# State-space stage of a decoder layer: convolution taps read the projection's bank, SiLU by ScalarE's own function, more banks for the projection, another order of the scan

## What is computed

```
h = rmsnorm(x, ln1_w)
z, xs, Bs, Cs, dt = split(h @ w_in.T, [512, 640, 768, 1280])
xBC = silu(causal_conv4(concat(xs, Bs, Cs), conv_w) + conv_b)   # 768 channels, 4 taps
dt  = softplus(dt + dt_bias);   a = dt * -exp(A_log)            # 4 heads
L   = tril(exp(cumsum(a)[q] - cumsum(a)[k]))                    # one chunk of 128
Y   = ((C @ B.T) * L) @ (xs * dt) + D * xs                      # state before it is zero
x1  = x + ((Y * silu(z)) @ w_out.T)
```

## Time and profile before

| | value |
|---|---|
| median of 3 runs | 1024.9 us (1024.14 to 1027.17) |
| the profiled execution's own time | 1025.79 us |
| its span, first to last instruction | 1024.0 us |
| mean granted TensorE clock | 0.98 |
| PE busy | 973.0 us, 95% of the span |
| DVE busy | 597.0 us, 58% |
| ACT busy | 495.0 us, 48% |
| POOL busy | 411.2 us, 40% |

### The profile page before, as it was taken

How to read it: one execution, slowest core, us unless ns; L and a number is a source line. 1 busy time by engine, 2 the same in 40 slices (tenths; PEclk the granted TensorE clock), 3 DMA queues, 4 the chain that set the end, 5 groups by cost and what they waited for, 6 DMA issues and landing times.

```text
span 1024.0 us, 15445 instructions
## 1 busy us (share of the span) xinstructions
PE 973.0 (95%) x5010; PEld 806.2 (79%) x5010; DVE 597.0 (58%) x1361; ACT 495.0 (48%) x1380; POOL 411.2 (40%) x341
## 2 busy tenths in 40 slices
PE   4897999999999999899999999999999999999886
PEld 3664677788888888788888888888888888888772
DVE  3879465322212247566667666666666676657865
ACT  4634535122312245654655654655555555555544
POOL 3334646534334353343442442532623523533312
PEclk9999899999999999999999999999999999999995
DMA  6110115101110211011011020020110110100002
GB/s 214 42 42 0 42 42 167 55 7 61 61 61 4 99 62 55 22 42 42 21 41 41 20 82 0 20 82 0 26 77 0 61 41 12 50 0 0 1 1 83
DMA packets 12976, 45.58 MB, mean 45 GB/s; under 512 B 1617, under 2 KB 2257, under 8 KB 9873
## 3 DMA queue, kind: packets, MB, share of 16 engines
q1 hardware_dynamic: 12944, 45.20, 12.7%
HBM read 43.10 MB, written 2.10 MB: 44 GB/s over the span
## 4 chain that ended last, share of the span: by engine, by line
PE 86%; DVE 8%; issue 2%; ACT 2%; POOL 1%; DMA 1%; SPq 0%; ACTq 0%; DVEq 0%
PE bank L377 25%; PE bank L378 24%; PE bank L379 24%; PE bank L651 5%; PE bank L661 3%; DVE cbuf L1634 2%; PE bank L775 1%; PE bank L388 1%; DVE xbc L1650 1%; DVE bst L1810 1%; PE bank L638 1%; DMA res<-in_x 1%; PE bank L741 0%; DVE xn L1592 0%; DVE res L1710 0%
## 5 line engine op out<-in xcount | busy, mean ns | idle before, releaser
L377 PE MATMUL bank<-act_hi,w_hi 128*128 128x512 f32 x560 | 226.3, 404 | 4.2 <-ACT cbuf L875 2.3
L379 PE MATMUL bank<-act_hi,w_lo 128*128 128x512 f32 x560 | 220.3, 393 | 0.0
L378 PE MATMUL bank<-act_lo,w_hi 128*128 128x512 f32 x560 | 220.1, 393 | 0.0
L1503 POOL TENSOR_TENSOR pb<-pb,prec 128x512 f32<-128x512 f32 x64 | 66.7, 1042 | 310.1 <-DVE prec L1944 310.1
L1160 ACT ACTIVATE pb<-pb,nmax 128x128 f32<-128x128 f32 x256 | 99.7, 391 | 78.2 <-DVE nmax L1939 78.2
L377 PEld LDWEIGHTS bank<-act_hi,w_hi 128*128 128x128 f32 x560 | 106.4, 190 | 28.9 <-issue 7.5
L378 PEld LDWEIGHTS bank<-act_lo,w_hi 128*128 128x128 f32 x560 | 106.3, 190 | 23.4 <-issue 2.2
L379 PEld LDWEIGHTS bank<-act_hi,w_lo 128*128 128x128 f32 x560 | 106.1, 189 | 23.0
L377 PE MATMUL bank<-w_hi,ot_hi 128*128 128x512 f32 x256 | 105.0, 410 | 0.8 <-DVE res L1957 0.8
L379 PE MATMUL bank<-w_hi,ot_lo 128*128 128x512 f32 x256 | 100.9, 394 | 0.0
L378 PE MATMUL bank<-w_lo,ot_hi 128*128 128x512 f32 x256 | 100.4, 392 | 0.0
(11 more groups left out here) (193 smaller groups left out, 2105.8 us busy)
## 6 DMA issues: line engine op xcount, KB each, us to landing
raw_a<-in_w_q SPq DMA_DIRECT2D x8, 1024.0 KB, 4.8
raw_b<-in_w_o SPq DMA_DIRECT2D x8, 1024.0 KB, 4.8
raw_a<-in_w_gu SPq DMA_DIRECT2D x7, 1024.0 KB, 5.3
raw_b<-in_w_kv SPq DMA_DIRECT2D x8, 512.0 KB, 3.3
raw_b<-in_w_dn SPq DMA_DIRECT2D x7, 512.0 KB, 3.4
res<-in_x SPq DMA_DIRECT2D x8, 256.0 KB, 6.4
raw_b<-in_ctx_t SPq DMA_DIRECT2D x8, 256.0 KB, 3.6
xre<-in_x SPq DMA_DIRECT2D x2, 1024.0 KB, 6.8
```

Of the source, the lines that this page charges most:

```text
L377: mm(o, l_hi, r_hi, start=first, stop=False)
L378: mm(o, l_hi, r_lo, start=False, stop=False)
L379: return mm(o, l_lo, r_hi, start=False, stop=last)
L1503: TT(pb[:, jj % 2, :, :], pb[:, jj % 2, :, :], prec[:, jj % 2, :].unsqueeze(2).to_broadcast([P, GH, L]), ALU.mult).then_inc(p_norm, 1)
```

## The change

- **Taps.** `conv` reads the raw value from the projection's bank instead of `pre`. Since there is no zero column, a tap of shift s adds only to columns s to 127 of each sequence. ScalarE's copy into `pre` is gone, and `pre` with it. The halved weights and their setup go too.
- **SiLU.** ScalarE's own SiLU writes `xbc` from `cbuf` and `zt` from the bank. `conv_silu` and `z_silu` on VectorE are gone, as are the factors of two.
- **Banks.** The projection uses banks 0, 1, 4, 5 in the first half of the tokens and 0, 1 and for two steps 6 in the second, by the table `IN_BANK`. A convolution's bank is now free only when its taps are done (`conv_c`), where before it was free when ScalarE had read it (`conv_ev`).
- **Order.** `dt_in(0)`, `dt_out(0)` and `dt_out(1)` stand earlier on VectorE. On TensorE `in_step(18)` and `in_step(19)` stand ahead of `ssm1(4)`. The output steps, the residual additions and the pieces of the normalization in the second half are threaded in another order.

```diff
+        IN_BANK = [0, 1, 4, 5, 0, 1, 4, 5, 0, 1, 0, 1, 6, 0, 1, 6, 0, 1, 0, 1]
             def in_step(f):
-                if f >= 2:
-                    pn, pp = order[f - 2]
+                if f == 12:
+                    pe.wait_ge(dt_a, 2)
+                elif f >= 4:
+                    pn, pp = order[max(e for e in range(f) if IN_BANK[e] == IN_BANK[f])]
                     if pp < NCONV:
-                        pe.wait_ge(conv_ev, NCONV * pn + pp + 1)
+                        pe.wait_ge(conv_c, NCONV * pn + pp + 1)
                     else:
                         pe.wait_ge(z_out, NH * pn + pp - NCONV + 1)
...
             def in_evac(f):
-                    A(pre[:, q % 2, :, DCONV - 1:], bank[f % 2][:, :].rearrange("p (s n) -> p s n", s=HALF),
-                      ACT.Copy)
-                    A(cbuf[:, q % 3, :], bank[f % 2][:, :], ACT.Identity,
+                    A(cbuf[:, q % 3, :], bank[IN_BANK[f]][:, :], ACT.Identity,
...
-                    A(th[:, 0, :], bank[f % 2][:, :], ACT.Tanh, scale=0.5).then_inc(z_th, 1)
+                    A(zt[:, h, n * NTOK:(n + 1) * NTOK], bank[IN_BANK[f]][:, :], ACT.Silu).then_inc(z_out, 1)
-            def conv_tanh(q):
+            def conv_silu(q):
                 act.wait_ge(conv_c, q + 1)
-                A(th[:, 1 + q % 2, :], cbuf[:, q % 3, :], ACT.Tanh).then_inc(conv_th, 1)
+                A(xbc[:, q // NCONV, q % NCONV, :], cbuf[:, q % 3, :], ACT.Silu).then_inc(conv_out, 1)
...
             def conv(q):
                 for k in (2, 1, 0):
-                    t = STT(c, pre[:, q % 2, :, k:k + L], cw[:, p * DCONV + k:p * DCONV + k + 1], c,
-                            ALU.mult, ALU.add)
+                    late = DCONV - 1 - k
+                    t = STT(c[:, :, late:], raw[:, :, 0:L - late], chan_sb[:, p * DCONV + k:p * DCONV + k + 1],
+                            c[:, :, late:], ALU.mult, ALU.add)
...
-            def conv_silu(q):
-                STT(xbc[:, q // NCONV, q % NCONV, :], th[:, 1 + q % 2, :], 1.0, cbuf[:, q % 3, :],
-                    ALU.add, ALU.mult).then_inc(conv_out, 1)
-            def z_silu(i):
-                STT(zt[:, h, n * NTOK:(n + 1) * NTOK], th[:, 0, :], 1.0, bank[f % 2][:, :], ALU.add, ALU.mult)\
...
             ssm2(3)
             in_step(16)
             in_step(17)
+            in_step(18)
+            in_step(19)
             ssm1(4)
-            in_step(18)
+            pe.wait_ge(conv_c, 2 * NCONV)
+            out_step(0)
             ssm1(5)
-            in_step(19)
             ssm2(4)
-            pe.wait_ge(dt_a, 2)
-            out_step(0)
+            out_step(1)
             ssm1(6)
             ssm2(5)
-            out_step(1)
+            out_step(2)
             ssm1(7)
             ssm2(6)
-            out_step(2)
+            out_step(3)
             ssm2(7)
-            out_step(3)
```

More of the change, by code:

```diff
@@ L407, in in_step @@
                     tok = slice(n * NTOK, (n + 1) * NTOK)
-                    t = mm3(bank[f % 2][:, :], w_hi[:, c0:c0 + P], w_lo[:, c0:c0 + P],
+                    t = mm3(bank[IN_BANK[f]][:, :], w_hi[:, c0:c0 + P], w_lo[:, c0:c0 + P],
                             act_hi[:, k, tok], act_lo[:, k, tok], k == 0, k == KT - 1)
@@ L931, in _ @@
             in_evac(2)
-            conv_tanh(1)
+            dt_exp(0)
+            conv_silu(0)
+            conv_silu(1)
             win_hi(6)
-            dt_exp(0)
             square(5)
             in_evac(3)
-            conv_tanh(2)
+            conv_silu(2)
             win_hi(7)
@@ L940, in _ @@
             in_evac(4)
-            conv_tanh(3)
+            conv_silu(3)
             win_hi(8)
@@ L944, in _ @@
             in_evac(5)
-            conv_tanh(4)
+            conv_silu(4)
             norm_hi(4, nb)
@@ L964, in _ @@
             dt_exp(1)
-            conv_tanh(7)
+            conv_silu(6)
             in_evac(12)
+            conv_silu(7)
             x_evac(2)
             decay(2)
-            conv_tanh(8)
             y_split(0)
@@ L973, in _ @@
             decay(3)
-            conv_tanh(9)
+            conv_silu(8)
+            in_evac(14)
             y_split(1)
-            in_evac(14)
-            conv_tanh(10)
+            conv_silu(9)
+            in_evac(15)
+            conv_silu(10)
             y_split(2)
-            in_evac(15)
             def wout_hi(k):
@@ L989, in _ @@
             wout_hi(1)
-            conv_tanh(11)
+            conv_silu(11)
             y_split(3)
@@ L1026, in _ @@
             gu_hi(0, 1)
+            square(9)
             y_split(5)
@@ L1601, in _ @@
             nb = (bank[2], bank[3])
-            V.memset(pre[:, :, :, :], 0.0).then_inc(setup_v, 1)
             V.memset(pow_m[:, :], -0.5).then_inc(setup_v, 1)
@@ L1748, in _ @@
             att_mul(1)
-            conv_silu(7)
-            conv(8, (y_out, 0))
+            y_out(0)
+            dt_out(1)
+            conv(8)
             att_mul(2)
             y_out(1)
-            conv_silu(8)
             conv(9)
@@ L1756, in _ @@
             y_out(2)
-            conv_silu(9)
-            conv(10, (y_out, 3))
-            dt_out(1)
-            conv_silu(10)
+            conv(10)
+            y_out(3)
             conv(11)
-            conv_silu(11)
-            z_silu(4)
-            z_silu(5)
+            add_res(0, 0, OUT_BANK[0])
             att_mul(4)
-            z_silu(6)
-            z_silu(7)
+            rms_var(8)
             att_mul(5)
             y_out(4)
-            add_res(0, 0, OUT_BANK[0])
-            rms_var(8)
-            y_out(5)
-            att_mul(6)
             add_res(1, 1, OUT_BANK[1])
@@ L1776, in _ @@
             rms_var(9)
-            y_out(6)
-            att_mul(7)
+            att_mul(6)
+            y_out(5)
             add_res(2, 2, OUT_BANK[2])
@@ L1781, in _ @@
             rms_var(10)
+            att_mul(7)
+            y_out(6)
+            add_res(3, 3, OUT_BANK[3])
             y_out(7)
-            add_res(3, 3, OUT_BANK[3])
             rms_x(10)
```

108 lines of the change are left out of this document (36 added, 72 removed).

## The result

The changed kernel takes 1016.92 us, the median of six runs (1013.68 to 1020.11), against 1023.87 us for six runs of the kernel before (1022.84 to 1027.17) on the same chip. The ratio is 0.9937, with a 95% interval from 0.9915 to 0.9960. It is faster by 7.0 us, where 14.6 us were forecast. The time lies within the stated range of 8 in 10 (1006.5 to 1018), whose upper end is that of rival 1, and outside the forecast's own range, which ends at 1014. Its median of 1011.33 us has it in and is 1010.67 without it.)

The account below looks back on a forecast made before the run. TensorE bounds the kernel, VectorE two stretches of the state-space stage. Winnable 16.7 us less 2.1 us of new waits gives 14.6 us: 1024.9 to 1010.3 us; own range 1007 to 1014, 8 in 10 range 1006.5 to 1018.

Parts of the forecast that it names:

- rival 1: Six ScalarE table loads lie on TensorE's path, costing 7.8 us; gain 6.8 us, 1018 us; chance 0.17.
- The bound and the pool: VectorE bounds two state-space stretches; TensorE's waits, 13.0 us, with hidden wait and lower clock make 16.7 us winnable.
- the last term of the new waits: Hand-overs around sequence 4 and at the scan's end, att_mul(7) behind y_split(5): 0.8 us of new TensorE wait.
- `dt_out(1)`: Placed ahead of taps 8 on VectorE, it makes attention products 2 and 3 come late: 0.5 us of new wait.
- Taps: 36 convolution taps on VectorE, read from the bank, take 750 ns instead of 1055: 11 us less.
- The 15.0 us of SiLU: VectorE loses its SiLU passes, 9.5 us at L1650 and 5.5 us at L1658; ScalarE does them at no extra cost.
- Table loads: Six more on ScalarE at 1.28 us, 7.7 us in all, partly hidden; the one ahead of sequence 4 most exposed.
- `dt_step(1)`: On TensorE it waits for norm_lo(7), now behind dt_out(0) on VectorE: a new wait of 0.6 us.
- Gates 16 and 17: In the second half, projection pieces 18 and 19 wait for these, which ScalarE empties behind y_split(3): 0.2 us.
- This takes that wait even if VectorE were no faster: in_step(18) and (19) ahead of ssm1(4) put 5.4 us of matmuls where TensorE stood 4.54 us for SiLU 11.
- Rivals 2 and 3: 2: waits return elsewhere, nothing is left, 1024 to 1026 us, chance 0.05; 3: slow bank taps, about 1032 us, 0.04.

Follow-up runs that it names:

- rsqrt9_early: Changed kernel with GpSimd doing rsqrt(9) right behind rsqrt(8), ahead of y_rest(5), decay_out(7) and gu_rest(0, 1): 1011.33 us, ratio 0.9891 to the kernel before.
- order_only: Kernel before the change with only in_step(18) and in_step(19) moved ahead of ssm1(4) on TensorE: 1024.33 us, ratio 1.0001.
- dt_out1_late: Changed kernel with dt_out(1) behind conv(11) on VectorE and GpSimd's decay_in(4), (5) behind wout_rest(3): 1017.53 us, ratio 0.9938 to the kernel before.

## Why the prediction was right and where it failed

**The bound and the pool held.** VectorE's queue was what TensorE waited for, the two stretches opened as computed, and with the order mended the kernel has 133.99 - 120.81 = 13.2 us less in the stage, of which 0.9 us is a head that happened to be short: 12.3 us. 14.6 were forecast. What could be won was sized well.

**The step that failed is the last term of the new waits,** "around sequence 4 [...] and at the end, where `att_mul(7)` waits behind `y_split(5)`, I take 0.8 us". At the end it measured 4.77 us, and for another reason. I had counted what the moved steps issue and took from that queue the hand-overs between the scan's own steps. I didn't ask of the norm's steps that now stand between them what they wait for: `rms_x(9)` had moved past `y_out(6)` and `att_mul(7)`, and GpSimd's order, which the change does not touch there, delivers its `rstd` at 119.4 us. The term lacks 4 us of wait and 2 us of lower clock: the L452 pair 0.9 us (2.05 for 1.13), the transposes 0.5 us (1.06 for 0.60), and the first matmuls behind them, as the granted clock of 0.77 from 125 to 130 us shows. rsqrt9_early takes this away, down to a wait of 2.02 us, and gains 4.7 us in the tail; that is the difference between 14.6 and 7.5 but for 2.4 us.

**The remaining 2.4 us.** rsqrt9_early still has 4.7 us of waits where I took 2.1, 2.6 us more, which is the size of what remains. Half of the excess is `dt_out(1)`, for which I took 0.5 us and which cost 1.48 + 0.32 us in the changed kernel, with `yb` as the name on it:

```profile
80.34 1.10 PE L452 MATMUL bank<-att,xtok 128*128 128x512 f32 x2 [1.48 <-DVE yb L1673]
...
84.52 0.67 PE L452 MATMUL bank<-att,xtok 128*128 128x512 f32 x1 [0.32 <-DVE yb L1673]
```

The chain that took 3.0 us for index 0 before takes 5.1 for index 1 (below). The other half is what is left of the wait at the end, 2.02 us for 0.8.

**Term by term.** Taps: 750 ns taken, 740 measured; right, and taking them back with the copy costs 8.2 us, as much as the change's whole measured gain. The 15.0 us of SiLU were never taken away alone, so their worth is not shown. The Trainium skill (SBUF — State Buffer, Who interferes with whom) says that a VectorE instruction with two inputs in SBUF contends with a GpSimd instruction that reads SBUF; the trace agrees, by 1055 to 741 ns in the mean when one of the two moved to a bank, and the tap's longest from 1775 to 748. Table loads: 1.28 us each as read, hidden but for 1.2 us; rival 1, with 7.8 us, has the right final time (1018 for 1016.92) by luck and is refuted as a mechanism, since without the loads the ratio is the same (0.9945 for 0.9938). The Trainium skill (ScalarE: Activation LUTs, What ACT_TABLE_LOAD costs) adds a drain of about 1380 ns; no trace here shows one. `dt_step(1)`: 0.6 taken, 0.73 measured. Gates 16 and 17: 0.2 taken, no wait shown. "This takes that wait even if VectorE were no faster" was wrong: order_only moved the wait and made it 5.3 us. Rivals 2 and 3 fell. Two sums were off: the range's lower end, 1006.5, is 16.7 and 0.8 below the span of 1024.0 and not below the median of 1024.9, which gives 1007.4; and rival 3's 1032 is not its own sum, since 11 us more than 1024.9 are 1036.

**What would have shown it beforehand.** The order of the instructions gives `rms_x(9)` ahead of `att_mul(7)` on VectorE and `rsqrt(9)` behind `decay_out(7)` on GpSimd. `decay_out(7)` is a supplier of `att_mul(7)` itself: so the product was certain to be ready before the norm that stood ahead of it. No duration is needed to see that the order is upside down.

**Left open.** What sets the end of the program to 121 or 124.5 us, and where the dips of the clock behind the stage fall. What the move of SiLU is worth by itself, and how the 8.2 us divide among taps, copy and banks.

## What to carry to other kernels

When an instruction is moved forward on one engine, look up what it waits for on the others, and whether that supplier moved with it; a step of a side chain placed ahead of the main chain turns its supplier's place in a third queue into a wait of the bounding engine. Price a bound engine's relief and its order apart: here the faster taps with the copy gone carried 8 us, the two projection steps moved alone none, and one misplaced step ate 4.7. And compare kernels by short stretches as well as by the total, since one profiled execution overstated this gain by 5 us; even the stage held 0.9 us of an early phase of the clock that no edit had touched.

## What the hardware showed that I had not expected

**Small VectorE instructions stop for a whole GpSimd instruction.** `dt_out(1)` in the changed kernel, VectorE, and GpSimd beside it:

```profile
72.06 3.59 DVE L1650 SCALAR_TENSOR_TENSOR sp<-sp 128x16 f32<-128x16 f32 x7
```

```profile
72.05 1.29 POOL L1357 TENSOR_TENSOR em<-em,md 128x512 f32<-128x512 f32 x1 [3.91 <-ACT em L906]
73.30 1.27 POOL L1316 TENSOR_TENSOR y_lo<-yb,y_hi 128x512 fp32r<-128x512 f32 x1
```

```profile
L1650 DVE SCALAR_TENSOR_TENSOR sp<-sp x14: 174/176/1311, 50.1 to 75.5; 128x16 f32<-128x16 f32 x14
```

Seven instructions of 128x16 take 3.59 us. In the kernel before the same seven, of `dt_out(0)`, took 1.43 us, with GpSimd idle beside them:

```profile
61.13 1.43 DVE L1681 SCALAR_TENSOR_TENSOR sp<-sp 128x16 f32<-128x16 f32 x7
```

```profile
63.06 2.04 POOL L1360 TENSOR_TENSOR md<-dt_sb,cst 128x512 f32<-128x512 f32 x2 [8.90 <-DVE dt_sb L1683]
```

In the changed kernel the median is 176 ns, the longest 1311, which is about the length of one GpSimd instruction. dt_out1_late, where `dt_out(1)` stands beside other GpSimd work, shows it more closely:

```profile
88.30 0.92 DVE L1646 TENSOR_TENSOR sp<-sp 128x16 f32<-128x16 f32 x1
89.25 1.21 DVE L1647 TENSOR_TENSOR sp<-sp 128x16 f32<-128x16 f32 x1
```

```profile
86.65 2.54 POOL L1316 TENSOR_TENSOR w_lo<-raw_b,w_hi 128x512 fp32r<-128x512 f32 x2
89.14 1.29 POOL L1316 TENSOR_TENSOR y_lo<-yb,y_hi 128x512 fp32r<-128x512 f32 x1
```

VectorE's instructions end at 89.22 and 90.46 us, each 0.03 us after one of GpSimd's (89.19 and 90.43). The norm's step shows the same: 0.74 us in rsqrt9_early, 1.74 us in the changed kernel beside GpSimd's L1316. In rsqrt9_early it started first, at 113.81 us, and there GpSimd's L1316 that started at 114.03 took 1.67 us instead of 1.28. So it looks like a stop of whichever comes second, and not like a slower rate; that is read from these few rows. No run was made for this question; the last two observations are the nearest to a test of it.
